# A quantised SwiGLU stage with its scales folded into the weights, read straight from PSUM, and with one clip moved to GpSimd

## The chip, the cores and the metric

The kernel runs on one core of a Trainium2 chip. The metric is the device time of one execution in microseconds. Three runs of the kernel before took 894.96, 893.86 and 894.86 us; their median is 894.86 us.

## The reference

The program is two layers of gated cross attention with a feed-forward part each, on 1024 tokens (16 x 64) of width 512. Only its last part is changed: layer norm of `x`, a quantised SwiGLU, and the gated residual.

```python
x_flat = layernorm(x).reshape(-1, 512).astype(bfloat16)
qg, sg = dynamic_quant(x_flat, inv_gate)     # xs = x * inv; s = max(max|xs| / 127, 1e-8)
qu, su = dynamic_quant(x_flat, inv_up)       # q = clip(round(xs / s), -127, 127)
gate_out = (qg @ w_gate.T) * sg * s_wgate[None, :]      # 256 columns
up_out   = (qu @ w_up.T)   * su * s_wup[None, :]
inter = clip(silu(gate_out) * up_out, -10, 10).astype(bfloat16)
qi, si = dynamic_quant(inter, inv_inter)
out = (qi @ w_down.T) * si * s_wdown[None, :]           # 512 columns
x = x + tanh(g_ffn[1]) * out
```

## The kernel before, in words

Four layers run one after the other, each in a block of its own with one program per engine; only the last block, `quantised_swiglu` (line 1354), is touched. `x` stays in SBUF as `x_sb`, 8 tiles of 128 tokens. The layers ahead leave the factor rows (`inv_gate`, `s_gate` and so on, spread over all partitions) in the ring `raw`, so they show as `raw` in the profile.

The block is a pipeline written out by hand over five stages: SMOOTH, QUANTISE, GATE_UP, INTER, DOWN are 0 to 4, and in step `s` the stage `n` works on tile `s - n`. `over` (line 1425) issues four filling steps, a loop of four steps and four draining steps. Each engine does in each step what its own `step` function lists, in that order. For tile `t`:

- VectorE normalises: `xb` (L1531, bf16). GpSimd multiplies it by the two rows `inv_gate`, `inv_up`: the pair `xs` (L1505).
- VectorE takes the largest magnitude of both halves (`am`, L1536), the scale `sc` (L1539) and its reciprocal `rs` (L1542). ScalarE multiplies and adds a large constant, which rounds: `qm` (L1454). VectorE clips `qm` in place, 1024 elements (L1546).
- TensorE transposes `qm` into the PSUM banks TG and TU (L1624), ScalarE copies them out as `q_t` (L1460), and TensorE multiplies by the gate and up weights into the bank GU (L1636). The weights are split in two parts, `wgu_hi` (ScalarE, L1490) and `wgu_lo` (VectorE, L1588), so 16 matmuls a tile.
- VectorE multiplies GU by the token scale and the column scale: `gu`, twice 256 elements (L1552, `scaled_gate_up`). ScalarE takes Silu of the gate half: `act_g` (L1475). VectorE multiplies both (`prod`, L1559) and clips (`ib`, L1561). GpSimd multiplies by `inv_inter`: `xi` (L1510). VectorE takes its maximum, scale, reciprocal and gate (`ami`, `sci`, `rsi`, `sdi`, L1566 to L1573).
- ScalarE rounds `qi` (L1470), VectorE clips it (L1577), TensorE transposes it into TI (L1644), ScalarE copies it as `qi_t` (L1465), TensorE multiplies by the down weights into DN (L1652).
- VectorE multiplies DN by the token scale and the column scale: `y` (L1583, `gated`). GpSimd adds `y` to `x_sb` (L1514), and SyncE stores the tile.

The weights come by three DMAs that SyncE issues at the start of the block. What sets the order of VectorE's work in a step is this list (before):

```python
if INTER in stages: scaled_gate_up(s - INTER, 1 - p)
if DOWN in stages: inner_clip(s - DOWN)
if QUANTISE in stages: scales(s - QUANTISE, 1 - p)
if INTER in stages: inner(s - INTER)
if SMOOTH in stages: normalize(s)
...
if DOWN in stages: gated(s - DOWN, p)
if QUANTISE in stages: clip(s - QUANTISE, 1 - p)
...
if INTER in stages: inner_scales(s - INTER)
```

Of the kernel before, what the change touches and what calls it, by code (L numbers as in the profile page):

```python
# [25 lines left out]
ALU = mybir.AluOpType  # L26
# [3 lines left out]
P = 128  # L30
# [1323 lines left out]
def quantised_swiglu(nc, d, c, out):  # L1354
# [15 lines left out]
    with ExitStack() as ctx:  # L1370
# [6 lines left out]
        def sem(name):  # L1377
# [13 lines left out]
        q_t = sb("q_t", [P, 2, KC, P], F32R)  # L1391
        gu = sb("gu", [P, 2, INNER])
        act_g = sb("act_g", [P, INNER])
# [8 lines left out]
        qi_t = sb("qi_t", [P, IC, P], F32R)  # L1402
        y = sb("y", [P, 2, D])
        TQ = [bank("TG"), bank("TU")]
# [4 lines left out]
        s_whi, s_wlo = sem("w_hi_ready"), sem("w_lo_ready")  # L1409
        s_magic, s_rstd = sem("magic_ready"), sem("last_rstd_ready")  # L1410
        s_xb, s_xs, s_am, s_sc, s_rs = (sem("xb_ready"), sem("xs_ready"), sem("amax_ready"), sem("scale_ready"),
                                        sem("inv_scale_ready"))
        s_qm, s_clip, s_t, s_qt, s_mm = (sem("quantised"), sem("clipped"), sem("t_done"), sem("q_t_ready"),
                                         sem("gate_up_done"))
        s_gu, s_act, s_prod, s_ib, s_xi = (sem("gate_up_scaled"), sem("silu_ready"), sem("product_ready"),
                                           sem("inter_ready"), sem("xi_ready"))
# [4 lines left out]
        s_y, s_x, s_out = sem("y_ready"), sem("x_final"), sem("out_stored")  # L1421

# [25 lines left out]
        def _(act):  # L1448
# [23 lines left out]

            def silu(t):
                act.wait_ge(s_gu, 2 * t + 1)
                nc.scalar.activation(act_g[:, :], gu[:, 0, :], ACT.Silu).then_inc(s_act, 1)  # L1475

            def step(s, p, stages):
                if INTER in stages:
                    silu(s - INTER)
                if DOWN in stages:  # L1480
                    inner_to_stationary(s - DOWN)
                if GATE_UP in stages:
                    to_stationary(s - GATE_UP)
                if QUANTISE in stages:
                    quantise(s - QUANTISE, 1 - p)
                if INTER in stages:
                    inner_quantise(s - INTER)
                if stages == STAGES[:2]:
                    act.wait_ge(s_wgu, 32)
                    nc.scalar.activation(wgu[0][:, :, :, :], wgu_raw[:, :, :, :], ACT.Copy).then_inc(s_whi, 1)  # L1490
                    act.wait_ge(s_wd, 16)
                    nc.scalar.activation(wd[0][:, :, :], wd_raw[:, :, :], ACT.Copy).then_inc(s_whi, 1)
# [3 lines left out]
        @block.gpsimd  # L1496
        def _(pool):
            nc.gpsimd.tensor_tensor(rstd[:, TILES - 1:TILES, 0], c["veps"][:, TILES - 1:TILES],
                                    c["mhalf"][:, TILES - 1:TILES], ALU.pow).then_inc(s_rstd, 1)
            pool.wait_ge(s_rows, 96)  # L1500

            def smooth(t, p):
                pool.wait_ge(s_xb, t + 1)
                for n in range(2):
                    nc.gpsimd.tensor_tensor(xs[:, p, n, :], xb[:, :], inv_gu[n], ALU.mult)\  # L1505
                      .then_inc(s_xs, 1)

            def inner_smooth(t):
                pool.wait_ge(s_ib, t + 1)
                nc.gpsimd.tensor_tensor(xi[:, :], ib[:, :], inv_in, ALU.mult).then_inc(s_xi, 1)  # L1510

            def add(t, p):
                pool.wait_ge(s_y, t + 1)
                nc.gpsimd.tensor_tensor(x_sb[:, t, :], x_sb[:, t, :], y[:, p, :], ALU.add).then_inc(s_x, 1)  # L1514

            def step(s, p, stages):
                if INTER in stages:
                    inner_smooth(s - INTER)
                if SMOOTH in stages:
                    smooth(s, p)  # L1520
                if DOWN in stages:
                    add(s - DOWN, p)

            over(step, pool.Fori)

        @block.vector
        def _(dve):
# [15 lines left out]

            def clip(t, p):
                dve.wait_ge(s_qm, 2 * t + 2)
                nc.vector.tensor_scalar(qm[:, p, :, :], qm[:, p, :, :], ROUND + QMAX, ROUND - QMAX,  # L1546
                                        ALU.min, ALU.max).then_inc(s_clip, 1)

            def scaled_gate_up(t, p):
                dve.wait_ge(s_mm, t + 1)  # L1550
                for n in range(2):
                    nc.vector.scalar_tensor_tensor(out=gu[:, n, :], in0=GU[p][:, n * INNER:(n + 1) * INNER],  # L1552
                                                   scalar=sc[:, p, n:n + 1], in1=sw_gu[n],
                                                   op0=ALU.mult, op1=ALU.mult).then_inc(s_gu, 1)

            def inner(t):
                dve.wait_ge(s_gu, 2 * t + 2)
# [21 lines left out]

            def gated(t, p):  # L1580
# [9 lines left out]
            def step(s, p, stages):  # L1590
                if INTER in stages:
                    scaled_gate_up(s - INTER, 1 - p)
                if DOWN in stages:
                    inner_clip(s - DOWN)
                if QUANTISE in stages:
                    scales(s - QUANTISE, 1 - p)
                if INTER in stages:
                    inner(s - INTER)
                if SMOOTH in stages:
                    normalize(s)  # L1600
                if stages == STAGES[:3]:
# [15 lines left out]
        def _(pe):  # L1617
# [172 lines left out]
```

## Time and profile before

| | |
|---|---|
| median of three runs | 894.86 us (893.86 to 894.96) |
| profiled execution | span 893.8 us (no time of its own is kept beside it) |
| TensorE busy | 792.5 us (89%) |
| VectorE busy | 723.5 us (81%) |
| ScalarE busy | 382.5 us (43%) |
| GpSimd busy | 363.9 us (41%) |
| TensorE's granted clock in the last four of 40 slices | 7, 8, 9 and 6 tenths |
| last block | from 813.6 us to the end of the span |

The profile is one execution. Its times are counted from the start of the span, and busy time is the time in which an engine has an instruction in work. A row of a timeline gives start, duration, engine, source line, operation, the tile written and the tiles read, and in brackets how long the engine had been idle and which instruction ended that. `x2` in a row joins two neighbours of the same line.

### The profile page before, as it was taken

How to read it: one execution, taken by the hardware profiler on the slowest of the kernel's cores; microseconds unless marked ns; L12 is line 12 of the kernel's file. 1: busy time of each engine (PE TensorE's matmuls, PEld its weight loads, DVE VectorE, ACT ScalarE, POOL GpSimd, SP SyncE). 2: the span in 40 equal slices, each digit the busy share in tenths (PEclk: the TensorE clock that was granted, in tenths of full speed). 3: DMA queues.
4: the chain of work that ended last, by engine and by line, in shares of the span. 5: the costliest groups of instructions: out<-in, count | busy, mean ns of one | idle time of the engine just before them, and what ended most of it. 6: DMA issues, size and time to landing. Idle time of an engine off the chain costs nothing. (4 is left out here: it accounts for less than half of the span.)

```text
span 893.8 us, 13394 instructions
## 1 busy us (share of the span) xinstructions
PE 792.5 (89%) x4276; PEld 644.9 (72%) x4276; DVE 723.5 (81%) x1282; ACT 382.5 (43%) x1095; POOL 363.9 (41%) x300
## 2 busy tenths in 40 slices
PE   2899987977899999999999989999999999984764
PEld 1555653966688888778888878888887888873653
DVE  5898987879788888768888868888885988886994
ACT  2777774322343433434343334443433443243552
POOL 2777876233542532314433313353332432203562
PEclk9999999987999999999999999999999999997896
DMA  8210120110110211101021000111100102002001
GB/s 266 77 47 23 48 76 1 36 41 7 48 48 24 60 43 29 36 14 48 24 59 48 24 26 25 48 36 47 48 25 13 48 12 54 0 1 72 12 36 47
DMA packets 37443, 37.46 MB, mean 42 GB/s; under 512 B 2896, under 2 KB 27216, under 8 KB 37392
## 3 DMA queue, kind: packets, MB, share of 16 engines
q1 hardware_dynamic: 35168, 32.81, 12.7%
q10 hardware_dynamic: 2224, 3.94, 1.4%
q8 instruction: 36, 0.59, 0.3%
q14 instruction: 15, 0.12, 0.0%
HBM read 34.64 MB, written 2.10 MB: 41 GB/s over the span
## 5 line engine op out<-in xcount | busy, mean ns | idle before, releaser
L917 POOL TENSOR_TENSOR dense<-rope_a,rope_b 128x512 f32<-128x512 f32 x62 | 79.4, 1280 | 236.9 <-DVE rope_b L1037 236.9
L971 ACT ACTIVATE ot_hi<-PB 128x512 fp32r<-128x512 f32 x64 | 38.3, 598 | 182.7 <-PE PB L1286 182.7
L962 ACT ACTIVATE e_sb<-masked,nmax 128x64 f32<-128x64 f32 x256 | 86.1, 337 | 70.3 <-DVE nmax L1068 70.3
L1202 PE MATMUL QB<-xT_hi,wq_lo 128*128 128x512 f32 x256 | 107.9, 421 | 1.7 <-DVE xT_lo L1113 1.7
L1202 PE MATMUL ROW<-wo_hi,ot_lo 128*128 128x512 f32 x256 | 103.5, 404 | 5.7 <-DVE ot_lo L1087 5.7
L1204 PE MATMUL QB<-xT_hi,wq_hi 128*128 128x512 f32 x256 | 101.9, 398 | 2.1 <-issue 2.1
L1203 PE MATMUL QB<-xT_lo,wq_hi 128*128 128x512 f32 x256 | 102.1, 399 | 0.0
L1203 PE MATMUL ROW<-wo_lo,ot_hi 128*128 128x512 f32 x256 | 101.9, 398 | 0.0
L1204 PE MATMUL ROW<-wo_hi,ot_hi 128*128 128x512 f32 x256 | 101.8, 398 | 0.0
L1077 DVE TENSOR_TENSOR p_dup<-e_sb,rz 128x512 f32<-128x512 f32 x64 | 98.8, 1543 | 2.2
L1037 DVE TENSOR_TENSOR rope_b<-QB,rope 64x512 f32<-64x512 f32 x124 | 85.3, 688 | 3.9
L1034 DVE TENSOR_TENSOR rope_a<-QB,rope 128x512 f32<-128x512 f32 x62 | 42.8, 690 | 47.5 <-PE QB L1204 47.5
L1301 PE MATMUL SB<-k_rot,dense 128*128 128x128 f32 x512 | 69.5, 279 | 9.4 <-POOL dense L917 7.6
L374 POOL TENSOR_TENSOR prob<-prob,rz 128x512 f32<-128x512 f32 x64 | 66.3, 1044 | 22.7 <-DVE rz L267 21.4
L1301 PEld LDWEIGHTS SB<-k_rot,dense 128*128 128x128 f32 x512 | 64.0, 194 | 12.9 <-issue 6.6
L1202 PEld LDWEIGHTS ROW<-wo_hi,ot_lo 128*128 128x128 f32 x256 | 48.6, 190 | 19.4 <-DVE ot_lo L1087 8.3
L1094 DVE SCALAR_TENSOR_TENSOR x_sb<-ROW,tg,x_sb 128x512 f32<-128x512 f32 x64 | 48.0, 751 | 17.9 <-PE ROW L1204 16.2
L771 POOL TENSOR_TENSOR wq_lo<-raw,wq_hi 128x512 fp32r<-128x512 f32 x32 | 41.7, 1304 | 49.9 <-ACT wq_hi L763 49.9
L192 ACT ACTIVATE prob<-RR,nmax 128x512 f32<-128x512 f32 x64 | 44.1, 689 | 34.5 <-DVE nmax L289 34.4
L1202 PEld LDWEIGHTS QB<-xT_hi,wq_lo 128*128 128x128 f32 x256 | 49.0, 191 | 13.4 <-issue 2.5
L1204 PEld LDWEIGHTS QB<-xT_hi,wq_hi 128*128 128x128 f32 x256 | 48.7, 190 | 11.8
L1204 PEld LDWEIGHTS ROW<-wo_hi,ot_hi 128*128 128x128 f32 x256 | 48.5, 190 | 11.9
(200 smaller groups left out, 2014.8 us busy)
## 6 DMA issues: line engine op xcount, KB each, us to landing
raw<-in_wq SPq DMA_DIRECT2D x32, 256.0 KB, 2.8
raw<-in_wo SPq DMA_DIRECT2D x32, 256.0 KB, 2.6
ctx_two<-in_ctx SPq DMA_DIRECT2D x16, 256.0 KB, 3.8
x_sb<-in_x SPq DMA_DIRECT2D x8, 256.0 KB, 7.9
ctx_raw<-in_ctxT ACTq DMA_DIRECT2D x1, 2048.0 KB, 13.4
raw<-in_wv SPq DMA_DIRECT2D x8, 256.0 KB, 2.8
raw<-in_wk SPq DMA_DIRECT2D x8, 256.0 KB, 2.9
out<-x_sb SPq DMA_DIRECT2D x8, 256.0 KB, 2.0
```

The costliest lines, as they stand in the source:

```text
L192: nc.scalar.activation(prob[:, u % 4, :], RR[u % 3][:, :], ACT.Exp, bias=nmax[:, u:u + 1], accum_out=zsum[:, u:u + 1])\
L374: nc.gpsimd.tensor_tensor(prob[:, u % 4, :], prob[:, u % 4, :], rz[:, u:u + 1].broadcast_to([P, D]), ALU.mult).then_inc(s_p, 1)
L917: nc.gpsimd.tensor_tensor(dst, a, b, ALU.add).then_inc(s_rot, 1)
L962: nc.scalar.activation(e_sb[:, r, :], masked[:, r, :], ACT.Exp, bias=nmax[:, r:r + 1], accum_out=zsum[:, r:r + 1]).then_inc(s_exp, 1)
L1034: nc.vector.tensor_tensor(a, v, cos.broadcast_to([P, 8, S]), ALU.mult).then_inc(s_parts, 1)
L1037: nc.vector.tensor_tensor(b[other], v[rows], sin[rows].broadcast_to([S, 8, S]), ALU.mult)\
L1077: nc.vector.tensor_tensor(p_dup[:, :, :, :], e_sb[:, :, :].unsqueeze(2).broadcast_to([P, 4, 2, S]), rz[:, :].unsqueeze(2).unsqueeze(3).bro ...
L1094: nc.vector.scalar_tensor_tensor(out=x_sb[:, tile, :], in0=OB[:, :], scalar=tg[:, 1:2], in1=x_sb[:, tile, :], op0=ALU.mult, op1=ALU.add)\
L1202: nc.tensor.matmul(out, lhs[1], rhs[0], start=first, stop=False)
L1203: nc.tensor.matmul(out, lhs[0], rhs[1], start=False, stop=False)
L1204: return nc.tensor.matmul(out, lhs[0], rhs[0], start=False, stop=last)
L1301: mm = nc.tensor.matmul(out[:, :, 2 * b + r, :], q, keys.rearrange("p (kb k) -> p kb k", kb=2), start=True, stop=True)
```

## The change

- The column scales `s_gate`, `s_up`, `s_down` are multiplied into the raw weights on GpSimd (`fold_scales`: two multiplies for gate and up, one for down, each of 128x1024), ahead of the split into two parts. ScalarE's `wgu_hi` and `wd_hi` wait for them.
- `gu` is gone. ScalarE's Silu reads the gate half of GU in PSUM, with the token scale as the activation's scale. VectorE's product reads the up half in PSUM and multiplies by the token scale and `act_g` in one instruction.
- VectorE's `inner` stands ahead of `scales` in the step.
- The clip of `qm` moves from VectorE to GpSimd, after `xs` in a step.
- `gated` writes `x_sb` directly (DN times scale plus `x_sb`); `y` and the add on GpSimd are gone.
- GpSimd's steps are written out and not looped.

```diff
@@ scalar
+            def silu(t, p):
+                act.wait_ge(s_mm, t + 1)
+                nc.scalar.activation(act_g[:, :], GU[p][:, 0:INNER], ACT.Silu, scale=sc[:, p, 0:1])\
+                  .then_inc(s_act, 1)
...
                 if stages == STAGES[:2]:
-                    act.wait_ge(s_wgu, 32)
+                    act.wait_ge(s_fold, 2)
                     nc.scalar.activation(wgu[0][:, :, :, :], wgu_raw[:, :, :, :], ACT.Copy).then_inc(s_whi, 1)
-                    act.wait_ge(s_wd, 16)
+                    act.wait_ge(s_fold, 3)
@@ gpsimd
-            def add(t, p):
-                pool.wait_ge(s_y, t + 1)
-                nc.gpsimd.tensor_tensor(x_sb[:, t, :], x_sb[:, t, :], y[:, p, :], ALU.add).then_inc(s_x, 1)
+            def clip(t, p):
+                pool.wait_ge(s_qm, 2 * t + 2)
+                nc.gpsimd.tensor_scalar(qm[:, p, :, :], qm[:, p, :, :], ROUND + QMAX, ROUND - QMAX,
+                                        ALU.min, ALU.max).then_inc(s_clip, 1)
+
+            def fold_scales():
+
+                pool.wait_ge(s_wgu, 32)
+                for n in range(2):
+                    nc.gpsimd.tensor_tensor(wgu_raw[:, n, :, :], wgu_raw[:, n, :, :],
+                                            sw_gu[n].unsqueeze(1).broadcast_to([P, KC, INNER]), ALU.mult)\
+                      .then_inc(s_fold, 1)
+                pool.wait_ge(s_wd, 16)
+                nc.gpsimd.tensor_tensor(wd_raw[:, :, :], wd_raw[:, :, :],
+                                        sw_d.unsqueeze(1).broadcast_to([P, IC, D]), ALU.mult).then_inc(s_fold, 1)
 
             def step(s, p, stages):
                 if INTER in stages:
                     inner_smooth(s - INTER)
                 if SMOOTH in stages:
                     smooth(s, p)
-                if DOWN in stages:
-                    add(s - DOWN, p)
-
-            over(step, pool.Fori)
+                if s == 0:
+                    fold_scales()
+                if QUANTISE in stages:
+                    clip(s - QUANTISE, 1 - p)
+
+            for s in range(TILES + len(STAGES) - 1):
+                step(s, s % 2, [n for n in STAGES if 0 <= s - n < TILES])
@@ vector
+            def inner(t, p):
                 dve.wait_ge(s_act, t + 1)
-                nc.vector.tensor_tensor(prod[:, :], act_g[:, :], gu[:, 1, :], ALU.mult).then_inc(s_prod, 1)
+                nc.vector.scalar_tensor_tensor(out=prod[:, :], in0=GU[p][:, INNER:2 * INNER],
+                                               scalar=sc[:, p, 1:2], in1=act_g[:, :],
+                                               op0=ALU.mult, op1=ALU.mult).then_inc(s_prod, 1)
...
-                nc.vector.scalar_tensor_tensor(out=y[:, p, :], in0=DN[:, :], scalar=sdi[:, 0:1],
-                                               in1=sw_d, op0=ALU.mult, op1=ALU.mult).then_inc(s_y, 1)
+                nc.vector.scalar_tensor_tensor(out=x_sb[:, t, :], in0=DN[:, :], scalar=sdi[:, 0:1],
+                                               in1=x_sb[:, t, :], op0=ALU.mult, op1=ALU.add).then_inc(s_x, 1)
...
             def step(s, p, stages):
-                if INTER in stages:
-                    scaled_gate_up(s - INTER, 1 - p)
                 if DOWN in stages:
                     inner_clip(s - DOWN)
+                if INTER in stages:
+                    inner(s - INTER, 1 - p)
                 if QUANTISE in stages:
                     scales(s - QUANTISE, 1 - p)
-                if INTER in stages:
-                    inner(s - INTER)
...
-                if QUANTISE in stages:
-                    clip(s - QUANTISE, 1 - p)
```

GpSimd at the start of the block, before:

```order
L1498 TENSOR_TENSOR rstd<-veps,mhalf 128x1
L1505 TENSOR_TENSOR xs<-xb,raw 128x512 x6
L1510 TENSOR_TENSOR xi<-ib,inv_in 128x256
L1505 TENSOR_TENSOR xs<-xb,raw 128x512 x2
L1430 UNCONDITIONAL_BRANCH
```

and now:

```order
L1497 TENSOR_TENSOR rstd<-veps,mhalf 128x1
L1504 TENSOR_TENSOR xs<-xb,raw 128x512 x2
L1520 TENSOR_TENSOR wgu_raw<-wgu_raw,raw 128x1024 x2
L1524 TENSOR_TENSOR wd_raw<-wd_raw,raw 128x1024
L1504 TENSOR_TENSOR xs<-xb,raw 128x512 x2
L1513 ISA
L1513 TENSOR_SCALAR qm<-qm 128x1024
L1504 TENSOR_TENSOR xs<-xb,raw 128x512 x2
L1513 TENSOR_SCALAR qm<-qm 128x1024
L1509 TENSOR_TENSOR xi<-ib,inv_in 128x256
```

The three multiplies of the weights stand between the pair `xs` of tile 0 and that of tile 1, and the clips of `qm` stand behind the pairs of the tile that follows.

VectorE in the first step of the loop (s = 4), before:

```order
L1552 SCALAR_TENSOR_TENSOR gu<-GU,sc,raw 128x256 x2
L1576 REGISTER_ALU
L1577 TENSOR_SCALAR qi<-qi 128x256
L1535 ISA
L1536 TENSOR_REDUCE am<-xs 128x2
L1539 TENSOR_SCALAR sc<-am 128x2
L1542 RECIPROCAL rs<-sc 128x2
L1557 ISA
L1559 TENSOR_TENSOR prod<-act_g,gu 128x256
L1561 TENSOR_SCALAR ib<-prod 128x256
```

and now:

```order
L1580 TENSOR_SCALAR qi<-qi 128x256
L1559 REGISTER_ALU
L1560 SCALAR_TENSOR_TENSOR prod<-GU,sc,act_g 128x256
L1564 TENSOR_SCALAR ib<-prod 128x256
L1549 ISA
L1550 TENSOR_REDUCE am<-xs 128x2
L1553 TENSOR_SCALAR sc<-am 128x2
L1556 RECIPROCAL rs<-sc 128x2
```

`gu` is gone, and the product and the clip `ib` of tile `s - 3` have moved ahead of the reduction of tile `s - 1`.

## Rows read from the trace of the kernel before

**Rows 1.** Busy time by engine in a stretch: us and instructions, then clock, DMA.

```profile
840.00:860.00 20.00, 12.89 (x86) 10.61 (x85) 19.56 (x41) 8.82 (x18) 13.53 (x11) 0.98 0.07 26
```

(The columns after the stretch and its length are PE, PEld, DVE, ACT, POOL, then the granted clock as a share of full speed, the DMA share and GB/s.)

**Rows 2.** Timeline of VectorE in one full step, 857.9 to 868 us.

```profile
857.95 0.86 DVE L1552 SCALAR_TENSOR_TENSOR gu<-GU,sc,raw 128x256 f32<-128x256 f32 x2
...
859.31 1.21 DVE L1536 TENSOR_REDUCE am<-xs 128x2 f32<-128x1024 f32 x1
...
860.92 0.42 DVE L1559 TENSOR_TENSOR prod<-act_g,gu 128x256 f32<-128x256 f32 x1
861.38 0.29 DVE L1561 TENSOR_SCALAR ib<-prod 128x256 bf16<-128x256 f32 x1
861.65 0.55 DVE L1531 TENSOR_SCALAR xb<-x_sb,mv,rstd 128x512 bf16 x1
...
862.77 1.64 DVE L1546 TENSOR_SCALAR qm<-qm 128x1024 f32<-128x1024 f32 x1
...
866.74 1.21 DVE L1536 TENSOR_REDUCE am<-xs 128x2 f32<-128x1024 f32 x1
```

**Rows 3.** Groups of instructions: count, busy us, mean ns, idle before.

```profile
L1514 POOL TENSOR_TENSOR x_sb<-x_sb,y 128x512 f32 (+1 forms) x8 | 10.1, 1268 | 9.3 <-DVE y L1583 9.3
L374 POOL TENSOR_TENSOR prob<-prob,rz 128x512 f32<-128x512 f32 x64 | 66.3, 1044 | 22.7 <-DVE rz L267 21.4
L1475 ACT ACTIVATE act_g<-gu 128x256 f32<-128x256 f32 x8 | 3.3, 415 | 2.6 <-DVE gu L1552 2.0
L1470 ACT ACTIVATE qi<-xi,magic,rsi 128x256 f32<-128x256 f32 x8 | 4.8, 601 | 20.8 <-DVE rsi L1572 20.8
```

**Rows 4.** Timeline of the first steps of the block, and the weight's DMA to landing.

```profile
814.07 0.50 SPq L1439 DMA_DIRECT2D wgu_raw<-in_w_upT  x1
...
wgu_raw<-in_w_upT SPq DMA_DIRECT2D x1, 512.0 KB, 5.8
...
818.89 2.29 POOL L1505 TENSOR_TENSOR xs<-xb,raw 128x512 f32<-128x512 bf16 x2 [2.18 <-DVE xb L1531]
819.90 1.91 ACT L1490 ACTIVATE wgu_hi<-wgu_raw 128x2048 fp32r<-128x2048 f32 x1
820.01 1.72 DVE L1546 TENSOR_SCALAR qm<-qm 128x1024 f32<-128x1024 f32 x1 [1.20 <-ACT qm L1454]
...
821.84 2.29 DVE L1588 TENSOR_TENSOR wgu_lo<-wgu_raw,wgu_hi 128x2048 fp32r<-128x2048 f32 x1
...
822.69 1.06 PE L1624 MATMUL TU<-ident,qm 128*128 128x128 f32 x4
...
824.28 0.59 ACT L1460 ACTIVATE q_t<-TU 128x512 fp32r<-128x512 f32 x1
...
826.02 1.22 DVE L1588 TENSOR_TENSOR wd_lo<-wd_raw,wd_hi 128x1024 fp32r<-128x1024 f32 x1
826.19 3.66 POOL L1505 TENSOR_TENSOR xs<-xb,raw 128x512 f32<-128x512 bf16 x2 [5.01 <-DVE xb L1531]
...
829.89 1.22 DVE L1536 TENSOR_REDUCE am<-xs 128x2 f32<-128x1024 f32 x1 [0.20 <-POOL xs L1505]
```

**Rows 5.** Gate and up of tiles 0 and 1: PE, PEld, DVE, clock, DMA.

```profile
824.90:828.80 3.90, 3.75 (x16) 3.49 (x16) 0.00 (x0) 0.50 0.02 4
832.00:834.30 2.30, 2.13 (x16) 1.96 (x16) 0.00 (x0) 1.00 0.00 0
```

**Rows 6.** Timeline of the last 14 us.

```profile
879.66 0.48 DVE L1552 SCALAR_TENSOR_TENSOR gu<-GU,sc,raw 128x256 f32<-128x256 f32 x1
...
880.05 0.28 DVE L1577 TENSOR_SCALAR qi<-qi 128x256 f32<-128x256 f32 x1
...
880.39 0.44 PE L1644 MATMUL TI<-ident,qi 128*128 128x128 f32 x2 [1.17 <-DVE qi L1577]
...
883.86 0.41 DVE L1566 TENSOR_REDUCE ami<-xi 128x1 f32<-128x256 f32 x1
...
889.90 1.26 POOL L1514 TENSOR_TENSOR x_sb<-x_sb,y 128x512 f32<-128x512 f32 x1 [4.63 <-DVE y L1583]
```

More of the change, by code:

```diff
@@ L1391, in quantised_swiglu @@
         q_t = sb("q_t", [P, 2, KC, P], F32R)
-        gu = sb("gu", [P, 2, INNER])
         act_g = sb("act_g", [P, INNER])
@@ L1402, in quantised_swiglu @@
         qi_t = sb("qi_t", [P, IC, P], F32R)
-        y = sb("y", [P, 2, D])
         TQ = [bank("TG"), bank("TU")]
@@ L1410, in quantised_swiglu @@
         s_magic, s_rstd = sem("magic_ready"), sem("last_rstd_ready")
+        s_fold = sem("w_scaled")
         s_xb, s_xs, s_am, s_sc, s_rs = (sem("xb_ready"), sem("xs_ready"), sem("amax_ready"), sem("scale_ready"),
@@ L1414, in quantised_swiglu @@
                                          sem("gate_up_done"))
-        s_gu, s_act, s_prod, s_ib, s_xi = (sem("gate_up_scaled"), sem("silu_ready"), sem("product_ready"),
-                                           sem("inter_ready"), sem("xi_ready"))
+        s_act, s_prod, s_ib, s_xi = sem("silu_ready"), sem("product_ready"), sem("inter_ready"), sem("xi_ready")
         s_ami, s_sci, s_rsi, s_sdi = (sem("inter_amax_ready"), sem("inter_scale_ready"),
@@ L1420, in quantised_swiglu @@
                                             sem("qi_t_ready"), sem("down_done"))
-        s_y, s_x, s_out = sem("y_ready"), sem("x_final"), sem("out_stored")
+        s_x, s_out = sem("x_final"), sem("out_stored")
         block = ctx.enter_context(nc.Block())
@@ L1471, in inner_quantise @@
                                      scale=rsi[:, 0:1]).then_inc(s_qi, 1)
-            def silu(t):
-                act.wait_ge(s_gu, 2 * t + 1)
-                nc.scalar.activation(act_g[:, :], gu[:, 0, :], ACT.Silu).then_inc(s_act, 1)
+            def silu(t, p):
+                act.wait_ge(s_mm, t + 1)
+                nc.scalar.activation(act_g[:, :], GU[p][:, 0:INNER], ACT.Silu, scale=sc[:, p, 0:1])\
+                  .then_inc(s_act, 1)
             def step(s, p, stages):
                 if INTER in stages:
-                    silu(s - INTER)
+                    silu(s - INTER, 1 - p)
                 if DOWN in stages:
@@ L1542, in scales @@
                 nc.vector.reciprocal(rs[:, p, :], sc[:, p, :]).then_inc(s_rs, 1)
[L1544 to L1557, printed above, removed]
+            def inner(t, p):
                 dve.wait_ge(s_act, t + 1)
-                nc.vector.tensor_tensor(prod[:, :], act_g[:, :], gu[:, 1, :], ALU.mult).then_inc(s_prod, 1)
+                nc.vector.scalar_tensor_tensor(out=prod[:, :], in0=GU[p][:, INNER:2 * INNER],
+                                               scalar=sc[:, p, 1:2], in1=act_g[:, :],
+                                               op0=ALU.mult, op1=ALU.mult).then_inc(s_prod, 1)
                 dve.wait_ge(s_prod, t + 1)
@@ L1578, in inner_clip, with gated @@
                                         ALU.min, ALU.max).then_inc(s_clipi, 1)
-            def gated(t, p):
+            def gated(t):
                 dve.wait_ge(s_sdi, t + 1)
                 dve.wait_ge(s_dn, t + 1)
-                nc.vector.scalar_tensor_tensor(out=y[:, p, :], in0=DN[:, :], scalar=sdi[:, 0:1],
-                                               in1=sw_d, op0=ALU.mult, op1=ALU.mult).then_inc(s_y, 1)
+                nc.vector.scalar_tensor_tensor(out=x_sb[:, t, :], in0=DN[:, :], scalar=sdi[:, 0:1],
+                                               in1=x_sb[:, t, :], op0=ALU.mult, op1=ALU.add).then_inc(s_x, 1)
             def weights_rest(n, lo, raw, hi):
@@ L1603, in step @@
                     weights_rest(1, wd[1][:, :, :], wd_raw[:, :, :], wd[0][:, :, :])
-                    dve.wait_ge(s_rows, 96)
                 if DOWN in stages:
-                    gated(s - DOWN, p)
-                if QUANTISE in stages:
-                    clip(s - QUANTISE, 1 - p)
+                    gated(s - DOWN)
                 if stages == STAGES[:2]:
@@ L1630, in gate_up @@
                 if used:
-                    pe.wait_ge(s_gu, 2 * t - 2)
+                    pe.wait_ge(s_prod, t - 1)
                 pe.wait_ge(s_qt, 2 * t + 2)
```

## The prediction

> **What bounds the kernel now.** The change touches only the last stage, so I first read how much of the span that stage is. The profile's first part says that TensorE is busy 89% of the span and VectorE 81% (the table above), but those are averages over four layers. The weights of this stage are requested at 813.6 us and the span ends at 893.8 us, so 80 us are in question. The table by stretches shows that in the steady part of this stage (840 to 860 us) VectorE is busy 19.56 of 20 us, while TensorE has 12.9, GpSimd 13.5 and ScalarE 8.8 [rows 1]. VectorE is the bound there. It is less so in the first steps and in the last 14 us.
>
> The timeline of VectorE in one step [rows 2] shows its costliest instructions; between them lie only short ones and no wait. From one reduction `am` to the next it is 7.43 us (859.31 to 866.74). For tiles 2 to 7 the reductions start at 829.89 and 866.74 [rows 2, 4], with four between them, so five steps take 36.85 us. In a step the change removes from VectorE the two `gu` instructions (0.86) and the clip `qm` (1.64 here). It also reorders the rest. Whether that pays depends on what GpSimd and the waits at the start of the stage cost, so I walk the path of `am(2)` to `am(7)` and then the tail.
>
> **The clip moved to GpSimd.** No row shows a GpSimd instruction with one input tensor. Its two-input ones take 1.268 us for 512 elements (`x_sb`) and 1.044 with an operand that is one repeated value (`prob`) [rows 3]. Upper bound for 1024 elements: twice 1.268 = 2.54. Lower bound: VectorE's own clip. It began at 820.01 while GpSimd held to 821.18 (818.89 + 2.29) and ended at 821.73, so it needs 0.55 to 0.66 when nothing stops it [rows 4]. I take 1.2: half the two-input price, because `prob` against `x_sb` shows that GpSimd pays for what it reads, and it reads one tensor here. It is also what VectorE takes to read 1024 values once (1.21, `am`) [rows 2].
>
> The Trainium skill, GPSIMD Engine Reference, Engine selection, says that one-input instructions run roughly at line rate on GpSimd and two-input ones about twice as slow as on VectorE. Line rate at its 1.2 GHz would be an estimated 0.85 us, and the sum below would be 2.1 us smaller (897.3 instead of 899.4); no row here shows it.
>
> **The folds.** Three multiplies of 128x1024 are new on GpSimd, ahead of `xs(1)` in its queue. Each costs between 2.09 (2 x 1.044) and 2.54 [rows 3]. I take 2.2, since the scale operand is repeated as in `prob`. They can't start before the second weight has landed, 814.07 + 5.8 = 819.9 [rows 4]. Now the walk:
> - three folds: 819.9 + 6.6 = 826.5.
> - `wgu_hi` on ScalarE waits for two of them: 824.3 + 1.9 = 826.2. `wgu_lo` on VectorE (2.3) reads two SBUF tensors and asks for them before `xs(1)` does; it runs from 826.5 to 828.8. That two such instructions exclude each other is seen at 826.19: the pair of `xs` took 3.66 instead of 2.29 while VectorE ran `wd_lo` (826.02) and a clip [rows 4]. So `xs(1)` runs from 828.8 to 831.1. Before, it had ended at 821.18.
> - `clip(0)` behind it on GpSimd: 832.3. Before 821.73.
> - eight transposes at the lower clock, 2.0 (from the end of the clip at 821.73 to 823.75): 834.3. Copies `q_t`, 1.1: 835.4. Gate and up, 16 matmuls, 3.75 at granted clock 0.50 and 0.15 to start: 839.3 [rows 4, 5].
> - Silu straight from PSUM with the scale as a pointer. From SBUF without it 0.415, and `qi`, of the same size and with such a pointer, 0.601. Between these two I take 0.6: 839.9 [rows 3]. Its table load comes while ScalarE waits for the matmuls and costs nothing.
> - product (0.48, as one `gu` instruction, whose operands lie in the same memories) and clip `ib` (0.3): 840.7 [rows 2, 6].
>
> In the new order `inner` stands ahead of `scales` on VectorE, so `am(2)` is queued behind this product, although its own input `xs(2)` is there at about 835. It starts at 840.7 instead of 829.89: **+10.8 us**. The reorder is forced: `sc` is now read by the product and would be overwritten. What was cheap before, because `gu` had copied the numbers out, is now a wait at the head of a queue.
>
> **The steps.** VectorE's own work in a step falls from 7.4 to about 5.2 (less 0.86 and 1.2 to 1.6), so it no longer sets the step. The new cycle runs through GpSimd. From the end of a clip: the waiting `qi` clip on VectorE, which needs the ports GpSimd holds, ends 0.15 later; product 0.45; `ib` 0.3; reduction, scale and reciprocal 1.6 (859.31 to 860.92); `xb` 0.6 with the hand-over; the pair `xs` 2.3; the next clip 1.2 (its input, from ScalarE, is there sooner). Sum 6.6 us [rows 2, 4]. Next behind is the cycle over two steps through TensorE (transposes 1.1 at full clock, `TI` 0.4 and the copies 1.5, gate and up 2.3, silu 0.6, product and `ib` 0.75, scales 1.6, `xb` 0.6, `xs` 2.3, clip 1.2: 12.35), about 6.2 a step: 0.4 of cover a step, 0.8 to 0.9 in two [rows 5, 6]. Five steps of 6.6 take 33.0 instead of 36.85: **-3.9 us**.
>
> **The tail.** After `am(7)` the path up to TensorE's last transposes keeps its length (1.6 for scales, 1.6 quantise, 1.2 to 1.7 clip). Then two things go. `TI(6)` starts at 880.39, because the clip of `qi(6)` at 880.05 is queued behind `gu(7)`, which waits for the gate/up matmuls ending at 879.2; now that clip is first and `TI(6)` starts right after them, 1.1 earlier, and with it `DN(6)`, `gated(6)` and `ami(7)` queued behind it (883.86, though its own input is ready before). And the add on GpSimd (889.90, 1.26) is gone, 1.33 with its hand-over. **-2.4 us** [rows 6]. The product itself has the price of `gu`, and `gated` that of `y`: the tensor read from SBUF is another, the count is the same.
>
> **Sum**: 10.8 - 3.9 - 2.4 = +4.5 us on the span of 893.8. The median of the runs is 894.86, 1.1 above that span; the difference is carried over: **899.4 us**. About 0.2% (1.8 us) is what a measurement of this kernel can tell from no change.
>
> **The rivals.**
> 1. *The forecast*, slower by 4.5. For it: every engine that gains work in the prologue is on the path there. Against it: the unseen price of the GpSimd clip, which counts six times (`clip(0)` and five steps). Chance 0.50; alone 896.5 to 903.
> 2. *GpSimd pays the two-input price for the clip*, 2.5: 6 x 1.3 = 7.8 more, 907.2. GpSimd is then the bound (the pair `xs` 2.3 and the clip 2.5 in each step, and its waits for the scales). The rows have only such instructions, which speaks for it; that nothing but the reads distinguishes 1.044 from 1.268 speaks against. Chance 0.12.
> 3. *Not slower*: the ports don't collide, and the clip runs at the lower bound. Mechanism: `wgu_lo` doesn't hold `xs(1)` back (-2.3) and the clip costs 0.66 (6 x -0.54 = -3.2): 4.5 - 5.5 = -1.0, 893.9. With free ports it decides from a clip of 0.9 downward (4.5 - 2.3 - 1.8 = 0.4). Against it: the pair of 3.66, and the clip of 820.01, which ended 0.55 after GpSimd did. The Trainium skill, SBUF — State Buffer, Who interferes with whom, says that a VectorE instruction with two SBUF inputs or in a two-port mode and a GpSimd one that reads SBUF shut each other out for a whole instruction; the trace agrees (3.66 against 2.29), and by it this rival falls. Chance 0.12.
> 4. *TensorE's clock*. Gate and up took 3.75 at granted clock 0.50 and 2.13 at 1.00 [rows 5], and the transposes 2.0 against 1.1. Before, that lay beside VectorE's queue. Now the cycle through TensorE has 0.9 of cover: each tile at the lower level costs 2.5 - 0.9 = 1.6. Two such tiles: 902.6. The slices of the page show the granted clock at 7, 8, 9 and 6 tenths at the end of the span, so single tiles at the lower level occur. Chance 0.14.
> 5. *A cheap clip with collisions*: clip 0.85 (-2.1), folds 2.09 (-0.3), silu 0.42 (-0.2): +1.9, 896.8, at the edge of no change. Chance 0.12.
>
> **How the numbers follow.** The predicted time is that of the first, 899.4. The range takes in 3, 4, 5 and the lower part of 2: 893.5 to 906. Faster by over 0.2%: the lower half of 3 and what errors of the walk add, 0.10. Within 0.2%: the rest of 3, half of 5, and the edge of 1, 0.19. Slower: 0.71.
>
> **What would show it.** In the changed profile `am(2)` should start near 840.7 with VectorE idle some 5 us ahead of it, ended by ScalarE's silu; the three folds should run from 819.9 to 826.5; `am` to `am` should be 6.6 us with an idle time before the product; the GpSimd clip should last 1.2 us; from `am(7)` to the end 24.7 us instead of 27.1. Wrong would be: a clip outside 0.85 to 1.6; `am(2)` before 838; steps that stay at 7.4 or fall below 6; `xs(1)` running beside `wgu_lo`.

## The result, and the profile after

| | before | the change |
|---|---|---|
| median of 18 runs each, same chips | 894.53 us (890.73 to 898.41) | 900.06 us (895.17 to 903.90) |
| ratio to before, 95% interval | | 1.0058 (1.0044 to 1.0072) |
| profiled execution | span 893.8 | 897.88, its span 896.1 |
| busy TensorE, VectorE, ScalarE, GpSimd | 792.5, 723.5, 382.5, 363.9 | 790.5, 706.2, 383.4, 368.1 |

The change is slower by 0.58%, 5.2 us (0.0058 x 894.5); 4.5 were forecast. VectorE lost 17.3 us of work and the program became slower.

Three views of the changed kernel tell where the time went. The first is the chain of waits through the last stage; its columns are start, duration, engine, tile and line.

```profile
813.25 5.82 DMA wgu_raw<-in_w_upT
...
819.14 4.64 POOL wgu_raw L1520 x2
823.78 2.30 POOL wd_raw L1524
826.08 4.24 POOL xs L1504 x2
...
830.46 1.05 POOL qm L1513
...
831.55 1.12 PE TG L1622 x4
832.67 0.87 PE TU L1622 x4
833.56 1.09 ACT q_t L1458 x2
...
834.79 3.77 PE GU L1634 x16
...
838.58 0.48 ACT act_g L1473
...
839.09 0.49 DVE prod L1560
...
839.90 1.14 DVE am L1550
...
847.38 2.04 PE DN L1650 x4
849.43 2.57 PE GU L1634 x16
852.02 0.48 ACT act_g L1473
852.53 0.49 DVE prod L1560
...
853.25 1.22 DVE am L1550
```

It is the walk of the prediction, piece for piece, up to `am(2)`. Behind it the chain is no longer the one forecast: between `am(2)` and `am(4)`, 13.4 us apart, it goes through TensorE and leaves `am(3)` out, and the down matmuls DN stand in it.

The second is the timeline of VectorE with the reductions `am(2)`, `am(3)` and `am(4)`.

```profile
839.09 0.48 DVE L1560 SCALAR_TENSOR_TENSOR prod<-GU,sc,act_g 128x256 f32<-128x256 f32 x1 [5.50 <-ACT act_g L1473]
839.61 0.29 DVE L1564 TENSOR_SCALAR ib<-prod 128x256 bf16<-128x256 f32 x1
839.82 1.21 DVE L1550 TENSOR_REDUCE am<-xs 128x2 f32<-128x1024 f32 x1
...
844.83 0.69 DVE L1564 TENSOR_SCALAR ib<-prod 128x256 bf16<-128x256 f32 x1
845.44 1.20 DVE L1550 TENSOR_REDUCE am<-xs 128x2 f32<-128x1024 f32 x1
...
853.25 1.21 DVE L1550 TENSOR_REDUCE am<-xs 128x2 f32<-128x1024 f32 x1
```

`am(2)` starts 9.9 us later than before (829.89, [rows 4]), and 10.7 later counted from the start of the block, which this execution reached 0.8 us sooner. Its input was ready at 835.73, as the timeline of GpSimd shows:

```profile
819.14 4.64 POOL L1520 TENSOR_TENSOR wgu_raw<-wgu_raw,raw 128x1024 f32<-128x1024 f32 x2 [3.26 <-DMA wgu_raw<-in_w_upT]
...
826.04 4.32 POOL L1504 TENSOR_TENSOR xs<-xb,raw 128x512 f32<-128x512 bf16 x2
830.46 1.04 POOL L1513 TENSOR_SCALAR qm<-qm 128x1024 f32<-128x1024 f32 x1
832.54 3.19 POOL L1504 TENSOR_TENSOR xs<-xb,raw 128x512 f32<-128x512 bf16 x2 [1.04 <-DVE xb L1545]
```

The third is the table of busy time by stretches, with the columns of [rows 1]. From 840 to 860 us VectorE went from 19.56 to 15.95 busy, and TensorE's granted clock from 0.98 to 0.90. From 860 to 880 us the clock is 0.83 in both kernels. The change:

```profile
820.00:840.00 20.00, 7.18 (x32) 6.66 (x32) 6.48 (x9) 7.21 (x8) 15.65 (x10) 0.50 0.00 1
840.00:860.00 20.00, 13.30 (x86) 11.64 (x85) 15.95 (x36) 11.26 (x20) 12.71 (x13) 0.90 0.07 26
860.00:880.00 20.00, 15.96 (x94) 14.11 (x92) 12.74 (x34) 11.52 (x21) 9.07 (x9) 0.83 0.11 40
```

The kernel before, in the last of these stretches:

```profile
860.00:880.00 20.00, 15.15 (x80) 13.01 (x80) 16.36 (x38) 9.54 (x19) 8.83 (x8) 0.83 0.13 48
```

To compare kernels whose layers ahead took a little more or less, I cut the stage at four marks of the trace: the first `xb` of the block (the zero), `am(2)`, `am(7)`, the end.

| us | first `xb` to `am(2)` | the five steps to `am(7)` | sum of the steps | `am(7)` to end | stage |
|---|---|---|---|---|---|
| before | 16.2 | 6.90 7.55 7.54 7.43 7.43 | 36.9 | 27.1 | 80.1 |
| the change | 26.9 | 5.62 7.81 5.84 7.81 5.83 | 32.9 | 23.4 | 83.2 |
| difference | +10.7 | | -3.9 | -3.7 | +3.1 |

This is one execution each. That of the change is 2.2 us under the median of its runs, so some 2 us of the 5.2 are not in this profile, and the table can't place them. The layers ahead, which are the same code in all kernels, vary by more than that: over the fourteen profiles of this document the block starts between 810.7 and 816.4 us. The table says where in the block time went, and the ratios say how much it was.

### The profile page after: what moved, and what is told of

Its sections match the earlier page's. It is cut to its first block and busy times, and to the rows that moved or that the text cites. A ratio compares the mean times of both kernels' runs of the same rounds, so it can differ in the third digit from the quotient of the medians.

```text
span 896.1 us, 13345 instructions
## 1 busy us (share of the span) xinstructions
PE 790.5 (88%) x4276; PEld 645.6 (72%) x4276; DVE 706.2 (79%) x1258; ACT 383.4 (43%) x1095; POOL 368.1 (41%) x303
## 6 DMA issues: line engine op xcount, KB each, us to landing
ctx_raw<-in_ctxT ACTq DMA_DIRECT2D x1, 2048.0 KB, 12.5
```

## The experiments

Ratios are to the kernel before on the same chip, with their 95% intervals. "Against the change" is the difference of two ratios times 894.5 us; it is uncertain by 2 to 3 us, as both intervals enter. The stage columns are those of the table above, from each kernel's own profile.

| run | ratio | to `am(2)` | steps | sum | tail |
|---|---|---|---|---|---|
| 1 no folds | 0.9918 | 17.2 | 7.18 5.84 9.00 5.84 7.82 | 35.7 | 21.5 |
| 2 folds on VectorE | 0.9956 | 20.2 | 8.18 5.85 8.85 5.83 7.79 | 36.5 | 21.5 |
| 3 folds late | 1.0019 | 24.2 | 8.25 6.59 7.06 5.84 7.79 | 35.5 | 21.5 |
| 4 clip on VectorE | 1.0015 | 24.0 | 7.46 6.55 6.54 6.55 6.53 | 33.6 | 21.9 |
| 5 folds and clip on VectorE | 0.9956 | 20.3 | 7.46 6.56 6.54 6.55 6.54 | 33.7 | 21.9 |
| 6 clip twice | 1.0130 | 28.1 | 5.62 9.87 5.84 10.21 5.83 | 37.4 | 24.6 |
| 7 clock kept up | 1.0006 | 26.4 | 5.63 6.58 6.56 6.56 6.55 | 31.9 | 20.6 |
| 8 before, clip on GpSimd | 1.0017 | 16.5 | 7.63 7.00 8.36 5.74 9.99 | 38.7 | 24.4 |
| 9 `inner` after `scales` | 1.0007 | 23.0 | 7.46 6.84 5.72 6.77 5.72 | 32.5 | 23.5 |
| 10 folds on VectorE, clock up | 0.9957 | 21.2 | 8.25 7.55 5.84 6.56 6.55 | 34.8 | 20.6 |
| 11 before, clock up | 0.9985 | 16.6 | 6.98 7.54 7.56 7.43 7.87 | 37.4 | 24.1 |
| 12 both on VectorE, clock up | 0.9941 | 20.3 | 7.44 6.56 6.54 6.55 6.54 | 33.6 | 20.7 |

### 1 to 3: the folds

**1, no folds.** The raw weights are split as they landed, so this kernel leaves the column scales out of its result.

```diff
-                if s == 0:
-                    fold_scales()
@@ scalar
-                    act.wait_ge(s_fold, 2)
+                    act.wait_ge(s_wgu, 32)
```

> The change without the three multiplies of the weights on GpSimd (the column scales are left out of the computation). Theory A, the folds at the head of the stage are the loss: xs(1) follows xs(0) as before, am(2) starts near 830 instead of 839.8, the later steps keep their 5.6 and 7.8 us, so the time falls by 9.5 to 10.5 us against the change: about 890, ratio to the kernel before 0.994 to 0.996. Rival B, the clip on GpSimd in every step is the loss and the folds lie beside waits for the weights: falls by 0 to 3 us, ratio 1.002 to 1.006. Rival C, the product queued ahead of the scales is the loss: as B.

Measured: 0.9918 (0.9886 to 0.9950), 12.5 us against the change, a little more than expected. `am(2)` comes 9.7 us earlier. So the folds are the prologue's loss, and without them the rest of the change, taken together, is a gain of 0.8%. The steps were expected to keep their lengths and did not: the first went from 5.62 to 7.18, one long one to 9.00. That holds for runs 2 and 3 too: with an earlier `am(2)` the five steps sum to 35.5 to 36.5 us instead of 32.9. So 2.6 to 3.6 of the 3.9 us that the steps of the change save are gone in these three runs, and the terms of the sum are not independent.

**2, the folds on VectorE**, in the step in which it would otherwise wait for the weights.

```diff
@@ gpsimd step
-                if s == 0:
-                    fold_scales()
@@ vector step
                 if stages == STAGES[:2]:
+                    fold_scales()
                     weights_rest(0,
```

> The change with the three multiplies on VectorE, behind xb(1) in its queue, where the profile of the change shows it idle for 7.8 us (817.9 to 825.7). Theory A: the multiplies take 2.3 (both halves) and 1.2 us there instead of 4.6 and 2.3, and neither xs(1) nor clip(0) stands behind them. Weights at 819.1, both folds done at 821.4, the down fold at 822.6, wgu_hi at 823.3, wgu_lo at 825.6, gate and up of tile 0 from 826 instead of 834.8, am(2) near 832: falls by 6 to 8 us against the change, about 893, ratio to the kernel before 0.996 to 0.999. Rivals B and C: falls by at most 2 us, ratio 1.003 or more.

Measured: 0.9956 (0.9933 to 0.9979), 9.1 us against the change, 1 us more than the most that was expected, and faster than before. Chain of waits:

```profile
816.49 3.68 DVE wgu_raw L1585 x2
820.17 1.98 DVE wd_raw L1589
822.15 2.29 DVE wgu_lo L1578
824.44 1.14 DVE am L1537
```

The folds take 5.7 us in place of 6.9. `xs(1)` no longer stands behind them: it runs beside the first ones, from 815.83 to 819.09, and `clip(0)` follows it.

**3, the folds late on GpSimd**, behind `xs(1)` and `clip(0)`.

```diff
-                if s == 0:
-                    fold_scales()
                 if QUANTISE in stages:
                     clip(s - QUANTISE, 1 - p)
+                if s == 1:
+                    fold_scales()
```

> The change with the multiplies still on GpSimd but behind xs(1) and clip(0) in its queue instead of ahead of them. Theory A, with the queue as its mechanism: clip(0) ends near 820.8 instead of 831.5, the folds run from 820.8 to 827.8, wgu_lo ends near 829.7, gate and up of tile 0 starts at about 830 instead of 834.8: falls by 3 to 5 us against the change, ratio to before 1.000 to 1.003. If only the length of the folds counted and not what stands behind them, it would not move (ratio 1.006).

Measured: 1.0019 (0.9997 to 1.0040), as expected. The place of the folds in GpSimd's queue is worth 3.5 us (1.0058 against 1.0019), their engine 5.6 more (1.0019 against 0.9956).

### 4 to 6 and 8: the clip

**4, the clip back on VectorE**, ahead of `inner_scales` as before.

```diff
@@ gpsimd step
-                if QUANTISE in stages:
-                    clip(s - QUANTISE, 1 - p)
@@ vector step, after gated
+                if QUANTISE in stages:
+                    clip(s - QUANTISE, 1 - p)
```

> The change with the clip of qm back on VectorE, at its old place behind gated; folds and all else stay. Theory A: the clip on GpSimd costs 1.04 us and blocks little; back on VectorE it costs 0.6 to 1.3 us there, behind gated, which waits for the down matmuls: the same or slower than the change by 0 to 4 us, ratio to before 1.006 to 1.010. Rival B, the GpSimd clip is the loss: falls by 5 us or more, ratio 0.999 to 1.001.

Measured: 1.0015 (0.9996 to 1.0033). The same as the change or slower was expected; it is 3.8 us faster. The table says where: `am(2)` 2.9 earlier, the tail 1.5 shorter, the steps only 0.7 longer. VectorE's timeline:

```profile
822.69 0.69 DVE L1588 TENSOR_SCALAR qm<-qm 128x1024 f32<-128x1024 f32 x1 [1.20 <-ACT qm L1452]
...
851.05 0.88 DVE L1588 TENSOR_SCALAR qm<-qm 128x1024 f32<-128x1024 f32 x1 [0.26 <-ACT qm L1452]
```

`clip(0)` was done at 823.4, while GpSimd had just begun the folds (822.75). In the change it stood behind them and behind `xs(1)`, and tile 0's transposes with it. That cost was in the sum of the prediction as a part of the path, but I had put it down to the folds alone. And in the steady steps VectorE does the clip in 0.87 us, and all steps but the first are 6.55.

**5, folds and clip on VectorE**, edits 2 and 4 together.

> The change with both the folds and the clip of qm on VectorE. The last two runs fell by 9.1 and 3.8 us against the change, each alone. Theory A2, one and the same loss: both took clip(0) and xs(1) or clip(0) alone out from behind the folds, and what is left of the clip on GpSimd in the steps (6.8 us a step on average there, 6.55 with the clip on VectorE) is about 1 us: together 9 to 11 us against the change, ratio to before 0.993 to 0.996. Rival B2, the losses add up, since the clip on GpSimd costs something in every step: 13 us, ratio 0.991 or less.

Measured: 0.9956 (0.9937 to 0.9975), as theory A2 expected. Run 2 gave the same. The gains of 4 (3.8) and 2 (9.1) do not add up to 13: both remove the wait of `clip(0)` behind the folds, and `am(2)` comes at 20.3 us in run 5 and at 20.2 in run 2. Behind `am(2)` the profile of run 5 is 2.4 us shorter than that of run 2, with its even steps; the medians don't show it, and their intervals could hide it. With GpSimd idle the folds are short, as VectorE's timeline shows:

```profile
822.49 2.35 DVE L1583 TENSOR_TENSOR wgu_raw<-wgu_raw,raw 128x1024 f32<-128x1024 f32 x2
824.76 1.21 DVE L1587 TENSOR_TENSOR wd_raw<-wd_raw,raw 128x1024 f32<-128x1024 f32 x1
```

That is 1.2 us for each of the three against 2.34 on GpSimd.

**6, the clip twice on GpSimd.**

```diff
                 nc.gpsimd.tensor_scalar(qm[:, p, :, :], qm[:, p, :, :], ROUND + QMAX, ROUND - QMAX,
-                                        ALU.min, ALU.max).then_inc(s_clip, 1)
+                                        ALU.min, ALU.max).then_inc(s_clip1, 1)
+                pool.wait_ge(s_clip1, t + 1)
+                nc.gpsimd.tensor_scalar(qm[:, p, :, :], qm[:, p, :, :], ROUND + QMAX, ROUND - QMAX,
+                                        ALU.min, ALU.max).then_inc(s_clip, 1)
```

> The change with the clip on GpSimd done twice over the same tile (it changes nothing the second time): 1.04 us more for each of eight tiles. The prediction let the clip count six times (tile 0 and five steps): +6.2 us and hand-overs, ratio to before 1.012 to 1.014. Rival, the cycle over two steps through TensorE sets the pace: the clip counts once for tile 0, once in each of two and a half pairs of steps and once in the tail, about 4.5 times: +4.7 us, ratio 1.010 to 1.012. If GpSimd had slack in the steps, only tile 0 and the tail would count: +2 us, ratio 1.008.

Measured: 1.0130 (1.0103 to 1.0158), 6.4 us against the change for 1.12 us a clip (1.04 and 0.08 of hand-over). That is 5.8 clips, and the prediction counted six, but the intervals leave room for the rival's 4.5 as well, and the trace speaks for the rival. The short steps stay at 5.62 and 5.84, and the long ones grow from 7.81 to 9.87 and 10.21. The chain of waits passes the doubled clip once in a pair of steps and then TensorE:

```profile
862.41 1.05 POOL qm L1513
863.54 1.05 POOL qm L1516
...
867.18 2.05 PE DN L1653 x4
869.23 3.25 PE GU L1637 x16
```

This pair is 2.4 us longer than in the change: 1.12 for the added clip, and the rest is TensorE, whose matmuls ran at the lower clock for longer (gate and up 3.25 instead of 2.58). So the clip counts about four times, once ahead of `am(2)`, once in each of two pairs and once in the tail, and some 2 us of the 6.4 are TensorE's clock.

**8, the kernel before with its clip on GpSimd** (and GpSimd's steps written out).

> The kernel before with the clip of qm alone moved to GpSimd, between the pair xs and the add, and GpSimd's steps written out. No folds, gu and y as before. VectorE loses 1.2 to 1.6 us of its 7.43 us step; GpSimd goes from 4.7 to 5.7 us. Theory A: VectorE is the bound, so steps fall by 0.5 to 1.2 us and the whole by 2 to 5: ratio 0.995 to 0.998. Rival B, a clip on GpSimd costs more than it frees (ports held, waits for xs): the same or slower, ratio 1.000 to 1.004.

Measured: 1.0017 (1.0001 to 1.0034), where theory A had a gain and rival B had this. The 1.6 us a step taken from VectorE give nothing: the steps are 5.74 to 9.99 and sum to 38.7 instead of 36.9. Its chain of waits shows TensorE's matmuls at their longer duration:

```profile
860.76 2.05 PE DN L1653 x4
862.80 3.01 PE GU L1637 x16
```

So the move of the clip is of no use by itself, in either kernel.

### 7, 10, 11 and 12: TensorE's clock

**7, the change with transposes of a constant added on TensorE** into an unused PSUM bank, in its waits.

```diff
+        WARM = bank("WARM")
...
             def step(s, p, stages):
+                if stages == STAGES[:1]:
+                    warm(150)
+                if stages == STAGES[4:]:
+                    warm(20)
...
+                if p == 1 and SMOOTH in stages and GATE_UP in stages:
+                    warm(16)
```

> The change with transposes of the identity into an unused PSUM bank where TensorE waits: 150 ahead of tile 0, 16 after gate and up of tiles 1, 3 and 5, 20 ahead of the last transposes. Nothing that the kernel computes changes. Theory D, the lower clock lies on the path: transposes and gate/up of tile 0 fall from 2.0 and 3.7 us to 1.1 and 2.1, the down and gate/up matmuls behind the waits from 2.0 and 2.6 to 1.2 and 2.1 in each of three pairs of steps, the last TI and DN from 0.7 and 2.1 to 0.45 and 1.2: 2.5 + 3 x 1.3 + 1.1 = 7 us less, at least 4 if some of it is covered: ratio to before 0.998 to 1.002. Rival: the cycle through GpSimd sets the steps and TensorE has cover: only tile 0 and the tail fall, 3 us, ratio 1.002 to 1.004.

Measured: 1.0006 (0.9988 to 1.0024), 4.7 us against the change. The total is in the range of theory D. The work that counts is the same; 16 transposes went into every second step. The stretches:

```profile
840.00:860.00 20.00, 15.98 (x120) 14.19 (x120) 16.71 (x38) 11.86 (x23) 12.63 (x13) 1.00 0.07 27
860.00:880.00 20.00, 16.36 (x118) 14.25 (x117) 15.53 (x35) 11.71 (x23) 9.76 (x10) 1.00 0.10 39
```

The long steps fell from 7.81 to 6.56, the short ones, all but the first, rose from 5.84 to 6.56, and the tail lost 2.8. By the stage columns 0.5 us were won ahead of `am(2)`, 1.0 in the steps and 2.8 in the tail; theory D had put 2.5, 3.9 and 1.1 there. In the change TensorE's timeline shows what the added work took away:

```profile
859.15 0.65 PE L1622 MATMUL TG<-ident,qm 128*128 128x128 f32 x4 [2.45 <-POOL qm L1513]
...
861.02 0.77 PE L1650 MATMUL DN<-wd_lo,qi_t 128*128 128x512 f32 x1 [0.57 <-ACT qi_t L1463]
```

After a wait of 2.45 us the transposes still ran at the higher level (0.65), and the matmuls of DN behind them at the 1.2 GHz level, 2.05 for the four instead of 1.17 to 1.19; gate and up took 2.6 instead of 2.1. In run 7 the same place of the chain reads:

```profile
853.15 1.19 PE DN L1651 x4
```

**10, run 2 with such transposes (75 at the start).**

> Folds on VectorE (ratio 0.9956 alone) and TensorE kept busy in its waits (75 transposes ahead of tile 0, 16 behind gate and up of tiles 1, 3, 5, 20 ahead of the last ones; 4.7 us won on the change). The two act at different places of one path, except that gate and up of tile 0 is in both: ratio to before 0.990 to 0.993, about 887 us. If the clock was covered once the folds are gone, it stays at 0.995 to 0.996.

Measured: 0.9957 (0.9940 to 0.9975), no gain over run 2. A gain of 2 to 5 us was expected, and none if the clock was covered. The steps gained 1.7 and the tail 0.9, but `am(2)` came 1.0 later, and the added transposes themselves stood on the path at the lower clock, as the chain of waits shows:

```profile
844.63 2.54 PE WARM L1657 x16
847.18 0.44 PE TG L1623 x4
```

**11, the kernel before with transposes in its waits at the start and in the last steps** (those of run 7 without the 16, 75 at the start).

> The kernel before with the 75 transposes ahead of tile 0 and the 20 ahead of the last ones, none in the steps. There VectorE's queue sets the steps, so the clock in the first step is covered and only the tail gains: TI 0.7 to 0.45 and DN 2.05 to 1.17, 1.1 us: ratio 0.998 to 0.9995. If the first tile lay on the path in the kernel before too, 2.5 us more: ratio 0.996.

Measured: 0.9985 (0.9969 to 1.0000), as expected: only the tail is shorter, 24.1 instead of 27.1, and 0.5 are given back in the steps and 0.4 ahead of them. So the lower clock costs the kernel before something too, in its tail, though less (1.3 us against 4.7).

**12, run 5 with the same transposes as run 11.**

> Folds and clip on VectorE (ratio 0.9956 alone) with the 75 transposes ahead of tile 0 and the 20 ahead of the last ones, none in the steps, since its steps are even at 6.55 us and the granted clock stays up in them. Gained: transposes and gate/up of tile 0, 2.5 us, and the tail, 1.1 us: ratio 0.991 to 0.9935. It should equal the run with the folds alone on VectorE and the clock kept up to within 1.5 us.

Measured: 0.9941 (0.9921 to 0.9961), median 889.44, a little less of a gain than expected and the fastest of the complete kernels; its interval overlaps those of 2 and 5. The gain over 5 is 1.2 us in the tail; tile 0 gained nothing. It beats before by 5.3 us and the change by 10.5.

### 9: the order on VectorE

**9, `scales` ahead of `inner` again**, with four buffers for `sc` instead of two, so that nothing is overwritten. The steps of VectorE and ScalarE had to be written out for it.

```diff
-        sc = sb("sc", [P, 2, 2])
+        sc = sb("sc", [P, 4, 2])
@@ vector step
+                if QUANTISE in stages:
+                    scales(s - QUANTISE, 1 - p)
                 if INTER in stages:
                     inner(s - INTER, 1 - p)
-                if QUANTISE in stages:
-                    scales(s - QUANTISE, 1 - p)
```

> The change with the product and its clip back behind the scales on VectorE, as in the kernel before; the scales get four buffers for it, and the steps of VectorE and ScalarE are written out. Rival C, the reduction am(2) queued behind the product is what costs: am(2) starts near 836 instead of 839.8 and 3 us or more are won, ratio to before 1.002 or less. Theory A: it wins little, because ScalarE's quantise(2) stands behind silu(0) and the copies q_t(1) anyway and ends near 842.5: the clip of tile 2 moves by about 1 us, and in the steps the product now comes later on the cycle through TensorE: the same as the change within 1.5 us, ratio 1.004 to 1.008.

Measured: 1.0007 (0.9989 to 1.0026), 4.6 us against the change. Theory A, by which the order is worth nothing, fell, and rival C came out. VectorE's timeline:

```profile
837.23 1.22 DVE L1551 TENSOR_REDUCE am<-xs 128x2 f32<-128x1024 f32 x1 [2.18 <-POOL xs L1505]
...
840.55 0.48 DVE L1561 SCALAR_TENSOR_TENSOR prod<-GU,sc,act_g 128x256 f32<-128x256 f32 x1 [1.69 <-ACT act_g L1473]
```

`am(2)` now starts when `xs(2)` is there, 3.9 us earlier, with its product still 3 us away. Of this the first step gives back 1.8 (7.46 instead of 5.62). The long steps fell from 7.8 to 6.8, with the granted clock at 0.99 and 1.00 from 840 to 880 us, though they are still uneven. No kernel was run with only the loops written out, so how much of the 4.6 that is stays open.

## Why the prediction was right, point by point

- **Direction and size: right, the size in part by luck.** +5.2 measured, +4.5 forecast, 900.06 in 893.5 to 906. In the profiled executions the terms are +10.7, -3.9 and -3.7 against +10.8, -3.9 and -2.4: they sum to +3.1, less than the forecast, and the other 2 us of the 5.2 have no place in the block. Run 1 shows the cause of the first term on the chip: without the folds `am(2)` comes 9.7 us earlier.
- **The prologue: right, with errors that cancel.** Folds 2.34 each (2.2 taken), the pair `xs(1)` 4.32 including its wait for `wgu_lo` (it ended at 830.4, 831.1 forecast), the clip 1.04 (1.2), Silu from PSUM 0.467 (0.6); the product 0.48, as taken. The clip lies between the forecast's price and the 0.9 below which rival 3 would have decided; the free ports of rival 3 were not seen.
- **What made up the 10.8: put down wrongly in part.** The prediction named the folds and the reorder. Runs 3 and 4 show a third: `clip(0)`, which was free on VectorE, queued behind the folds. Taken back alone it gives 3.8 us.
- **"The reorder is forced": wrong.** It is forced with two buffers of `sc`. With four it isn't, and it costs up to 4.6 us (run 9). That `am(2)` is queued behind a product it doesn't need was read rightly; the prediction took it for unavoidable and counted nothing for the steps.
- **The steps: the sum right (33.0 forecast, 32.9 measured), the mechanism not.** They are not five of 6.6. They alternate, 5.8 and 7.8, and three of the five are short and two long; steps under 6 were one of the prediction's own signs of being wrong. At the mean of a pair five steps would take 34.1, so 1.2 us of the agreement is where the marks fall. The cycle through GpSimd is as walked when the clock is kept up: 6.56 in run 7, with the clip `qi` ending 0.15 after GpSimd's clip. In the short steps of the change `qi` slips in between `xs` and the clip, and the product, which reads PSUM, runs beside the clip, so 0.75 of product and `ib` fall out of the 6.6: 5.84. Then the other cycle has to catch up.
- **The clip: counted too often.** The prediction let it count six times. On the chain of the change it stands four times, at 830.46, 844.34, 857.98 and 871.62, once for two tiles, and the doubled clip of run 6 counts four times too.
- **The step of the sum that failed is "next behind is the cycle over two steps through TensorE, 12.35", where it takes full clock.** Measured are 13.65 for two steps (853.25 to 866.90), with DN 2.05 and gate and up 2.6 in it. At run 7's DN of 1.19 and the full-clock gate and up of 2.13 [rows 5] it would be 12.3. The length at full clock was therefore right, though DN stands where the prediction had the copies `q_t`, which run beside it. The cover of 0.9 was gone, and this cycle set the long steps. That is the condition of rival 4, in every pair; it cost 0.5 a pair against the 13.2 forecast, where the rival took 1.6 for a tile. Run 7 puts the whole price of the clock at 4.7 us, and by its profile most of that lies in the tail and only 1.0 in the steps.
- **The tail: mis-sized, -3.7 instead of -2.4.** From the last tile's transposes to the end it fell by 4.9. The add gave 1.4 (1.33 forecast). Because the clip of `qi(6)` is no longer queued behind `gu(7)`, `TI(6)` starts 0.63 after the matmuls instead of 1.17, 0.5 of the 1.1 forecast, and the DN of the tile before starts 1.0 sooner behind the transposes. The other 2.0 are DN and GU at full clock there (DN and the last gate and up took 4.6 us before, 874.63 to 879.23, and 3.1 now; the next DN 1.7 and 1.2). 1.2 were given back ahead of it, because these transposes were queued behind slow matmuls of the tile before.
- **What no run takes apart:** the reads from PSUM without `gu`, the add merged into `gated`, and GpSimd's steps written out. They are only in the 0.8% of run 1, together, and the written-out steps also in run 8, beside the clip.
- **Rule against row.** The Trainium skill, GPSIMD Engine Reference, Engine selection, has one-input instructions run roughly at line rate, which made an estimated 0.85 us for the clip; the row says 1.04, 1.2 times that. The rule of the Trainium skill, SBUF — State Buffer, Who interferes with whom, by which a VectorE instruction with two SBUF inputs and a GpSimd one that reads SBUF shut each other out for a whole instruction, holds in this trace: the pair `xs(1)` beside `wgu_lo` took 4.32 against 2.27 for the pair ahead of it.

The groups of the changed kernel that carry these prices (count, busy us, mean ns, idle before):

```profile
L1513 POOL TENSOR_SCALAR qm<-qm 128x1024 f32<-128x1024 f32 x8 | 8.3, 1042 | 4.3 <-ACT qm L1452 3.7
L1560 DVE SCALAR_TENSOR_TENSOR prod<-GU,sc,act_g 128x256 f32<-128x256 f32 x8 | 3.8, 479 | 7.1 <-ACT act_g L1473 7.0
L1473 ACT ACTIVATE act_g<-GU,sc 128x256 f32<-128x256 f32 x8 | 3.7, 467 | 2.4 <-PE GU L1634 2.4
```

## What to carry to other kernels

Work that is taken off the busiest engine has to land where nothing waits for it: 7 us of weight multiplies at the start of a stage cost more than five shorter steps and a shorter tail gave back, and the same multiplies on the engine that would have stood idle turned the loss into a gain. When a copy is removed by reading its source directly, ask which work now queues behind the later reader, and whether one more buffer lets the old order stand. And walk the cycle through TensorE with everything that stands in its queue and at both clock levels: at full clock it was 0.9 us short of setting these steps, and at the lower one it set them. Last, when a run agrees with a count, look in its trace where the time went: the doubled clip gave nearly the six clips that were counted, and a third of it was something else.

## What the runs showed of the hardware that was not expected

- A one-input, two-operation clip of 128x1024 takes 1.042 us on GpSimd; a two-input multiply of that size takes 2.34 there and 1.2 on VectorE while GpSimd is idle.
- The smallest VectorE instructions wait for a whole GpSimd one too. The gate `sdi`, 128x1 from two SBUF tensors, takes 0.14 us at its shortest and 1.10 beside the second `xs` of a pair; it ended at 857.91, the pair (855.60 and 2.29 long) at 857.89. VectorE's timeline of the change:

```profile
856.81 1.10 DVE L1576 TENSOR_TENSOR sdi<-sci,tg 128x1 f32<-128x1 f32 x1
```

- What TensorE's clock followed is not shown. In the change DN ran at the lower level behind each of three waits of 1.86, 2.45 and 2.35 us, though the transposes between were still at the higher one. In run 9, with uneven steps too, DN stayed at the higher level (1.18) behind a wait of 1.88 us:

```profile
858.37 0.65 PE L1624 MATMUL TG<-ident,qm 128*128 128x128 f32 x4 [1.88 <-POOL qm L1514]
```

- Even steps were no guard: with steps of 6.55 the granted clock from 860 to 880 us was 1.00 in run 4 and 0.91 in run 5, where one DN took 2.06 although no wait in these steps was above 0.9, and the kernel before had 0.83 with its even steps of 7.4. Run 5, TensorE's timeline:

```profile
862.25 0.76 PE L1650 MATMUL DN<-wd_lo,qi_t 128*128 128x512 f32 x1 [0.56 <-ACT qi_t L1463]
```
